# Eight graph convolutions on one core: the rows that prefill the next sums table go out from another queue, in larger pieces

## What is computed

```
x = layernorm(x + gcn(x))     # three layers: sum of weighted neighbours, @ W, + b, + x0, relu, batchnorm
x = layernorm(x + eve(x))     # two layers: relu(x @ wpool), max and min over neighbours, mixed, @ weve, + x @ wself + bias
x = layernorm(x + sage(x))    # two layers: mean over neighbours @ W_l, + x @ W_r + b, swish between
x = layernorm(x + gat(x))     # one attention layer: softmax over the edges of a destination
```

## Time and profile before

| | |
|---|---|
| median of three runs, without a profile | 10,876.99 us |
| span of the profiled execution | 15,443.7 us |
| seven convolutions together, in the profile | 5,041 + 6,717 us |
| degrees and what is ahead of it, `norm_nodes`, attention | 893, 565, 2,228 us |
| busy: PE, DVE, ACT, POOL | 7,253.9, 6,203.1, 4,646.1, 7,180.1 us |
| share of the 16 DMA engines: SP's queue, ACT's, POOL's | 32.9%, 11.2%, 8.7% |

### The profile page before, as it was taken

How to read it: one execution, slowest core, us unless ns; L and a number is a source line. 1 busy time by engine, 2 the same in 40 slices (tenths; PEclk the granted TensorE clock), 3 DMA queues, 4 the chain that set the end, 5 groups by cost and what they waited for, 6 DMA issues and landing times. The chain is left out here.

```text
span 15443.7 us, 165743 instructions
## 1 busy us (share of the span) xinstructions
PE 7253.9 (47%) x36946; PEld 5501.8 (36%) x36947; DVE 6203.1 (40%) x16108; ACT 4646.1 (30%) x8631; POOL 7180.1 (46%) x7582
## 2 busy tenths in 40 slices
PE   1024544454534448854455555533334445445553
PEld 0024444444534444333333333323333333223332
DVE  3333433343434335522222333322223333378887
ACT  1111111111211114422222333412223333266676
POOL 4654444444454441144444444355554444557663
PEclk9987777777767779977777777866666667667776
DMA  6965554666656667644444444545555555233333
GB/s 164 209 154 171 172 167 148 205 200 194 202 176 198 193 194 255 235 142 158 143 166 143 162 160 159 177 144 173 168 171 170 183 177 192 81 104 119 114 114 100
DMA packets 1864962, 2570.76 MB, mean 166 GB/s; under 512 B 255901, under 2 KB 1369141, under 8 KB 1864662
## 3 DMA queue, kind: packets, MB, share of 16 engines
q1 hardware_dynamic: 1134168, 1627.20, 32.9%
q10 hardware_dynamic: 504726, 564.87, 11.2%
q0 software_dynamic: 225792, 375.94, 8.7%
HBM read 1499.55 MB, written 1129.98 MB: 170 GB/s over the span
## 5 line engine op out<-in xcount | busy, mean ns | idle before, releaser
L1078 POOL DMA_INDIRECT sums_gcn<-m_result,m_idx x1176 | 1162.8, 989 | 2311.9 <-DVE m_result L1399 1952.8
L1220 ACT ACTIVATE m_nodeT<-m_n_bank 128x512 f32<-128x512 f32 x980 | 544.3, 597 | 4220.6 <-remote 2400.8
L1626 PE MATMUL m_gram<-m_y 128*128 128x129 f32 (+1 forms) x4800 | 900.6, 336 | 1765.6 <-issue 1462.9
L1683 DVE SCALAR_TENSOR_TENSOR m_acc<-m_n_bank,m_scales,m_res_b 128x128 f32<-128x128 f32 (+1 forms) x2352 | 644.9, 343 | 2569.6 <-remote 1864.2
L1078 POOL DMA_INDIRECT sums_eve<-m_result,m_idx x784 | 762.7, 973 | 1696.8 <-DVE m_result L1515 1470.9
L1187 PE MATMUL m_n_bank<-k_ident,m_in_y 128*128 128x128 f32 x5488 | 895.6, 321 | 1310.0 <-DVE m_z L1772 826.9
L1772 DVE TENSOR_TENSOR m_z<-m_n_bank,m_in_sums 128x512 f32<-128x512 f32 (+1 forms) x784 | 511.9, 687 | 2412.8 <-remote 1300.2
L1626 PEld LDWEIGHTS m_gram<-m_y 128*128 128x128 f32 (+1 forms) x4800 | 801.2, 245 | 1845.4 <-issue 1523.6
L1078 POOL DMA_INDIRECT sums_sage<-m_result,m_idx x784 | 762.7, 973 | 1375.9 <-DVE m_result L1399 1134.3
L1070 POOL DMA_INDIRECT m_rows<-node_rows_a,m_idx x1176 | 1124.4, 956 | 358.5 <-issue 338.1
L1187 PEld LDWEIGHTS m_n_bank<-k_ident,m_in_y 128*128 128x128 f32 x5488 | 754.1, 168 | 1437.8 <-DVE m_z L1772 902.7
(11 more groups left out here) (302 smaller groups left out, 17415.1 us busy)
## 6 DMA issues: line engine op xcount, KB each, us to landing
m_in_sums<-sums_gcn SPq DMA_DIRECT2D x291, 512.0 KB
m_in_y<-node_rows_a SPq DMA_DIRECT2D x291, 512.0 KB
sums_gcn<-k_gcn_b SPq DMA_DIRECT2D x194, 512.0 KB
node_rows_a<-m_y ACTq DMA_DIRECT2D x194, 512.0 KB
m_in_x<-in_x_dram SPq DMA_DIRECT2D x194, 512.0 KB
m_in_y<-node_rows_b SPq DMA_DIRECT2D x194, 512.0 KB
sums_eve<-k_eve_b SPq DMA_DIRECT2D x194, 512.0 KB
m_in_sums<-sums_eve SPq DMA_DIRECT2D x194, 512.0 KB
```

What stands on the lines that cost most here:

```text
L1078: pool.indirect_dma_start(self.node_sums[:, :], bass.IndirectOffsetOnAxis(self.idx[s][:, T + t:T + t + 1], 0), self.result[b][:, t, :], No ...
L1220: act.activation(out, src, ACT.Copy).then_inc(self.n_turn_read, 1)
L1626: mm = pe.matmul(self.gram[:, 0:D + 1], self.y1[b][0:rows[b], t, 0:D], self.y1[b][0:rows[b], t, :], start=False, stop=False, skip_group_ch ...
L1683: ins = dve.scalar_tensor_tensor(out=self.acc[b][0:n, tt, :], in0=ph.node_out(i, n)[:, t, :], scalar=self.scales[b][0:n, tt:tt + 1], in1=s ...
```

## The change

The two fills that SP issued behind the loads of each node pair are gone. In their place ACT issues one fill at the start of each edge unit, ahead of its own work of that unit: unit j fills rows 4096 j to 4096 j + 4095 of the next table, 32 rows from each partition. Unit 24 fills the 1,696 rows that are left, 16 rows from each of 106 partitions. Unit 25 fills nothing. The number of rows, their packets of 512 bytes and the wait at the end of the phase stay. The degrees phase, which already fills a table from ACT's queue in pieces of 1,024 rows, is not changed.

```diff
+FILL_ROWS = 4 * CH
...
-        if self.fill_table is not None:
-            for b in range(2):
-                c = m * 2 + b
-                n = self.sh.rows(c)
-                sp.dma_start(node_rows(self.fill_table, c, self.sh),
-                             spread_slots(self.fill_row[0:n, :], [n, T, D])).then_inc(self.filled, 16)
+    def fill_piece(self, act, j):
...
+        rows, whole = FILL_ROWS, self.sh.n // FILL_ROWS
+        if isinstance(j, int) and j > whole:
+            return
+        if isinstance(j, int) and j == whole:
+            rows = self.sh.n - whole * FILL_ROWS
+            part = self.fill_table[whole * FILL_ROWS:self.sh.n, :]
+        else:
+            part = self.fill_table[bass.ds(j * FILL_ROWS, FILL_ROWS), :]
+        each = rows // P if rows % P == 0 else 2 * T
+        act.dma_start(part.rearrange("(p j) f -> p j f", j=each),
+                      spread_slots(self.fill_row[0:rows // each, :], [rows // each, each, D])).then_inc(self.filled, 16)
...
-            sp.wait_ge(self.filled, 16 * self.sh.node_chunks)
+            sp.wait_ge(self.filled, 16 * (self.sh.n // FILL_ROWS + 1))
...
-            merged_sweep(act, k, sh, lambda *u: edges.scalar(act, *u), lambda *u: nodes.scalar(act, *u))
+            def edge_unit(j, *u):
+                ph.fill_piece(act, j)
+                edges.scalar(act, j, *u)
+
+            merged_sweep(act, k, sh, edge_unit, lambda *u: nodes.scalar(act, *u))
```

More of the change, by code:

```diff
@@ L58, in __init__ @@
         assert self.last_nodes % T == 0 and n_nodes < FAR
+        assert n_nodes // FILL_ROWS == self.edge_pairs and n_nodes % FILL_ROWS % (2 * T) == 0 < n_nodes % FILL_ROWS < 2 * CH
         self.last_rows = self.last_nodes // T
@@ L1164, in load_nodes @@
                              node_rows(self.streams[name], c, self.sh)).then_inc(self.landed[name][b], 16)
-        if self.fill_table is not None:
-            for b in range(2):
-                c = m * 2 + b
-                n = self.sh.rows(c)
-                sp.dma_start(node_rows(self.fill_table, c, self.sh),
-                             spread_slots(self.fill_row[0:n, :], [n, T, D])).then_inc(self.filled, 16)
+    def fill_piece(self, act, j):
+        if self.fill_table is None:
+            return
+        rows, whole = FILL_ROWS, self.sh.n // FILL_ROWS
+        if isinstance(j, int) and j > whole:
+            return
+        if isinstance(j, int) and j == whole:
[6 more added lines that the diff above has]
+                      spread_slots(self.fill_row[0:rows // each, :], [rows // each, each, D])).then_inc(self.filled, 16)
     def all_filled(self, sp):
         if self.fill_table is not None:
-            sp.wait_ge(self.filled, 16 * self.sh.node_chunks)
+            sp.wait_ge(self.filled, 16 * (self.sh.n // FILL_ROWS + 1))
     def have(self, eng, name, m, b):
```

## The result

The changed kernel takes 11,154.57 us (median of four runs, 11,132.02 to 11,160.46) beside 10,880.74 us for the kernel before on the same chip: a ratio of 1.0243, 95% interval 1.0229 to 1.0257. It is slower by 274 us. The forecast was 11,150 us, so the time came out as predicted. The reason did not: the step that carried the forecast shows in two of the 50 pieces of m1 and m2 and in none of m4 and m5, and something else made up the time.

A forecast was written before the change was run, and what follows sets the result against it. Convolutions were put at or somewhat above POOL's indirect-transfer floor, with the other engines' chain partly hidden: 10,877 + 325 (late ACT) - 50 (earlier loads) = about 11,150 us; own range 10,950 to 11,350, 8-in-10 range 10,740 to 11,560.

The forecast's parts named there:

- ACT held at the issue of the fill: Edge units of m1, m2, m4, m5: each whole piece delays ACT's activations, 651 us in all, half taken, +325 us.
- What leaves SP: SP's queue without its two fills per node pair: loads behind them start sooner, a gain of some 50 us.
- faster: Rival: loads freed from fills gain up to 3.0 us per node pair, ACT's wait hidden by POOL; 10,700 us, chance 0.18.
- m5, late by 8.7 us per unit: Edge units of m5: two more loads than m4 hold ACT 9.5 us, so its work comes 8.7 us late.
- m4, late by 6.5 us per unit: Edge units of m4: the piece's issue holds ACT 7.3 us, so its work comes 6.5 us late.
- m0, m6, m7 hidden: ACT's hold, at most 12.1 us in m0, 7.3 in m6 and 9.5 in m7, is covered and costs nothing.
- The last piece: 1,696 rows ending each table: issue does not wait, 0 us; the two-engine rule would allow 140 us at most.
- POOL's floor: POOL's indirect transfers take 1,010 to 1,030 us per convolution, a floor that hides part of the other engines' delay.
- Stores behind the rest of the piece: First node pair's stores on ACT's queue, behind 2,370 packets or 3.4 us: issued later than that, so no cost.
- The other signs: In the trace: SP's issues all under 2 us; POOL's gap grows about 7 us per unit in m1, m2, m4, m5.
- everything shows: Rival: the engines' chain exceeds POOL's floor in m1, m2, m4, m5, and the full 651 us counts; about 11,530 us, chance 0.18.
- no change: Rival: the engines' chain has room under POOL in every convolution, wait and relief vanish; 10,877 us, chance 0.13.

The follow-up runs named there:

- the fills ahead: The seven tables filled in a stage of their own on SP's queue ahead of m0, the convolutions issuing no fills: 12,465.99 us, one run.
- second profile of before: The kernel before, unchanged, profiled again because its first profile was stretched to 1.42 times the runs: 10,862.66 us, one run.
- the second tile: Stores of m0 to m2 in 4,096-byte packets from a tile ACT copies, wait moved to the copy: 10,920.33 us on the changed kernel, 10,893.99 on the kernel before.

## Why the prediction came out, and where it was wrong

- *ACT held at the issue of the fill, 651 us, half of it shown (+325).* This is the step that failed. A piece's issue took 0.6 to 0.9 us in the median, and "wrong I am if the issue of a whole piece takes 1 to 2 us" applies. In m1 the first activation of the edge unit came 4.5 us behind the stores (2177.93 to 2182.39), not 12. The limit of 2,370 packets read from the earlier trace rows is not a limit on a queue: in the fills ahead of the convolutions, with two pieces in the queue, an issue returned while about 5,400 were left. Nor is 690 packets per us the rate of a queue alone, as the earlier trace rows was read: it is that of two queues together, and whole pieces alone moved at 563. In place of this step m1 and m2 lost 241 us, 224 of them also with no fill on ACT at all (the fills ahead), to late stores, so that the sum came near the recorded one by chance. A unit of m1, from the first activation of one edge unit to that of the next, grew from 39.9 to 46.1 us in the mean of the first 16 with two node pairs each behind the start-up (the first edge units of a phase, which have no node pairs between them). Of this 4.2 lie in the node pairs and 1.8 between the last store and the first activation; with no fill on ACT both are there as well. The step had 7.2, all in the second place.
- *What leaves SP: a gain of 50 us.* The wrong sign. The loads behind the fills did start sooner, and that is what hurt: they took the turns that the fills had left to the stores. The earlier trace rows held the fact, 17.5% of the time for 512-byte packets beside large ones. I used it for the fill on ACT and for the rival "faster", not for the stores that were in that queue already.
- *m5, late by 8.7 us per unit.* It lost 1.8 us per unit, from 46.5 to 48.3, by the same average: 0.8 between the last store and the first activation (the issue itself), 0.5 in the edge unit, 0.5 in the node pairs. With the pieces on SP's queue it is 46.7. Whether the last two parts are contention was not tried. The 35 us are 42 lost in the 21 units behind the start-up, 7 of them in the last unit, less 6 gained in the start-up.
- *m4, late by 6.5 us per unit; m0, m6, m7 hidden.* m4's units took 39.7 us before and after, by the same average: ACT's 0.8 us more at the issue do not show. m0, m6 and m7 are as forecast. What each lost, 5 to 12 us, is about what the last piece gave back.
- *The last piece: 0 us by the rows.* Wrong; 6 us per phase in the ratios, 8 to 13 in the stages of five. The rule that was weighed against the rows, the Trainium skill's page "DMA: Bandwidth & Descriptors", section "Why a DMA increments its semaphore by 16 and not by 1", gave two engines for 106 partitions, and an estimate of 20 us from it; the trace agrees with 20.2 us on about two engines. Of the 140 us that it allowed at most, some 40 were on the path.
- *POOL's floor and the convolutions in the runs.* The floor was right: m4 and m6 stand on it with 1,022 us in the second profile of before. The seven take 1,064 us in the mean, inside the 1,027 to 1,183 worked out, but the middle, 1,105, was too high, and "half of it shown" had no ground but that middle. m1 and m2 (1,059 and 1,064) waited only 25 and 28 us at POOL for their results, yet nearly all of their units' 6 us came through; m0, with 1,053, hid its delay. How far a convolution stands above the floor did not tell which.
- *Stores behind the rest of the piece: nothing.* Right, as the empty queue shows.
- *The other signs.* SP's issues came out as forecast: none above 2 us in the convolutions after, 314 in the second profile of before. POOL's waits of over 1 us ahead of its scatters grew in m1 and m2 by 5 to 6 us per unit, near the 7 of the forecast and for another reason; in m4 and m5 by 0.2 and 1.5.
- The rivals: "everything shows" and "no change" are out by the ratio, "faster" by its sign. None named the stores.

## What to carry to other kernels

Before moving a transfer out of a queue, ask what runs beside that queue, not only what stands in it: where queues take turns packet for packet, a stream of small packets is slowed by every large packet next to it, and removing a small-packet stream from the load queue takes away the neighbour that cost it least. Cure the small packets themselves (here a store tile with one column too many), and the place of the fills hardly matters (with the second tile the ratio is 1.0027 with the fills on ACT, 0.9979 with them on SP). And when a profiled execution is 1.4 times as long as the runs, take another one before reading from it which waits are small.

## What the runs showed that was not expected

- Making fills larger (512 to 4,096 bytes per packet, same queue, place and bytes) made a kernel 4.35% slower; making loads smaller (4,096 to 512) made another 2% faster.
- What an issue waits for stays open. It returned with about 5,400 packets of its queue left when two pieces of 4,096 were in it, after 0.87 us with 5,400 left behind two stores (2178.39), and after 8.0 us with 5,700 left behind two stores that had hardly begun (2128.4). But with two stores and two fills of 1,024 each it held ACT until some 1,800 to 2,800 were left. So it isn't one number of packets for every transfer.
- One and the same program had waits for stores of 14 us in a stretched execution and 323 us in an ordinary one.
